# Cross and FFN attention scores from SBUF in fp32 at four row positions, in a three-layer decoder kernel on one Trainium2 core

## The reference

```python
scores = jnp.einsum('bhtd,bhsd->bhts', q, k) + bias      # cross; FFN: / sqrt(8), no bias
probs = jax.nn.softmax(scores, axis=-1)
attn = jnp.einsum('bhts,bhsd->bhtd', probs, v)
attn = attn.reshape(B, T, E)                             # cross: heads NOT moved back:
return attn @ Wo.T + bo                                  # row r of the result mixes 16 query rows of one head
```

## Time and profile before

| | us |
|---|---|
| median of 3 runs | 501.8 (501.21 to 505.19) |
| the profiled execution's own time | 496.74 |
| its span, first to last instruction | 495.0 |
| mean granted TensorE clock, share of full speed | 0.906 |
| busy: PE, weight load, DVE, ACT, POOL | 372.0, 313.7, 292.6, 197.8, 185.8 |

### The profile page before, as it was taken

The page is one execution under the profiler, slowest core; times in us unless marked ns, Lnnn a source line. Parts: engine busy times, 40 slices in busy tenths (PEclk is TensorE's granted clock), DMA queues, the critical chain, the costliest instruction groups (busy, mean ns, idle before and its releaser), DMA issues.

```text
span 495.0 us, 12557 instructions
## 1 busy us (share of the span) xinstructions
PE 372.0 (75%) x4671; PEld 313.7 (63%) x4683; DVE 292.6 (59%) x838; ACT 197.8 (40%) x390; POOL 185.8 (38%) x249
## 2 busy tenths in 40 slices
PE   1699997387699889978999984993886950039995
PEld 0244453257698788977988973982875930039994
DVE  5323334379768778687876764683783645007773
ACT  1266666043233423434335453461652720015552
POOL 6773412102324343244535544044030322723554
PEclk9999999589899999999999988896995985559998
DMA  7102357625976868776415368659496000332431
GB/s 177 31 3 86 98 171 186 168 73 139 242 187 180 206 182 221 207 189 181 122 47 156 110 173 222 170 147 226 118 253 176 3 0 22 106 98 57 106 92 30
DMA packets 60003, 66.34 MB, mean 134 GB/s; under 512 B 4373, under 2 KB 47384, under 8 KB 57640
## 3 DMA queue, kind: packets, MB, share of 16 engines
q1 hardware_dynamic: 49992, 45.61, 35.5%
q10 hardware_dynamic: 8448, 16.78, 12.3%
q0 software_dynamic: 1504, 3.16, 1.8%
HBM read 46.77 MB, written 19.22 MB: 133 GB/s over the span
## 4 chain that ended last, share of the span: by engine, by line
PE 42%; DMA 19%; DVE 15%; issue 9%; POOL 8%; SPq 3%; ACT 1%; POOLq 0%; DVEq 0%; ACTq 0%
PE score_banks L537 18%; DMA stack<-k_scratch 15%; PE proj_bank L537 7%; PE out_bank L537 5%; PE finish_bank L540 4%; DMA k_scratch<-parts 3%; PE prep_bank L537 3%; POOL routed_rows L520 3%; DVE biased L968 3%; DVE rowmax L972 2%; PE score_banks L540 2%; PE prep_bank L540 2%; POOL parts L380 2%; SPq L269 2%; DVE rest L946 2%
## 5 line engine op out<-in xcount | busy, mean ns | idle before, releaser
L537 PE MATMUL score_banks<-stack 72*128 72x128 bf16 x1024 | 134.1, 228 | 38.5 <-DMA stack<-k_scratch 37.0
L815 ACT ACTIVATE probs<-score_banks 128x512 f32<-128x512 f32 x128 | 76.4, 597 | 116.4 <-PE score_banks L537 115.3
L537 PEld LDWEIGHTS score_banks<-stack 72*128 72x128 bf16 x1024 | 86.7, 103 | 41.8 <-issue 38.6
L537 PE MATMUL score_banks<-maxT,pick 128*128 128x128 bf16 x512 | 93.9, 225 | 0.0
L424 POOL TENSOR_TENSOR att_sel<-att,in_block 128x1024 f32<-128x1024 f32 x16 | 34.4, 2150 | 78.6 <-DVE att L1004 78.6
L540 PE MATMUL score_banks<-ident,bias_in 128*128 128x128 f32 x256 | 62.0, 278 | 0.0
L977 DVE TENSOR_REDUCE rowmax<-score_banks 128x4 f32<-128x512 f32 x64 | 41.5, 682 | 23.1 <-PE score_banks L537 23.1
L537 PEld LDWEIGHTS score_banks<-maxT,pick 128*128 128x128 bf16 x512 | 52.2, 102 | 4.4
L367 POOL TENSOR_SCALAR vareps<-meanvar 128x2 f32<-128x2 f32 x32 | 7.2, 225 | 124.7 <-DVE meanvar L921 124.7
L968 DVE TENSOR_TENSOR biased<-score_banks,bias_in 128x512 f32<-128x512 f32 x64 | 43.7, 683 | 16.5 <-PE score_banks L537 15.9
L998 DVE RECIPROCAL rowsum_inv<-finish_bank 128x16 f32<-128x16 f32 x48 | 12.2, 255 | 68.4 <-PE finish_bank L540 68.2
(11 more groups left out here) (147 smaller groups left out, 655.2 us busy)
## 6 DMA issues: line engine op xcount, KB each, us to landing
k_scratch<-parts SPq DMA_DIRECT2D x48, 192.0 KB, 2.8
stack<-q_scratch SPq DMA_DIRECT2D x16, 576.0 KB
stack<-k_scratch SPq DMA_DIRECT2D x16, 576.0 KB
bias_in<-in_w SPq DMA_DIRECT2D x16, 256.0 KB, 8.2
q_scratch<-parts SPq DMA_DIRECT2D x16, 192.0 KB, 2.7
routed_rows<-filler SPq DMA_DIRECT2D x2, 1028.0 KB, 8.5
vaug<-routed_rows SPq DMA_DIRECT2D x23, 64.5 KB, 2.2
parts<-routed_rows SPq DMA_DIRECT2D x23, 64.0 KB, 2.1
```

Of the source, the lines that this page charges most:

```text
L537: return nc.tensor.matmul(o, lhsT, rhs, start=start, stop=stop, **kw)
L815: nc.scalar.activation(probs[:, b % 2, g, :], sbk[g % 2], ACT.Exp, scale=1.0 if layer(b) == CROSS else SCALE).then_inc(s_p, 1)
```

## The change

- The scratch round trip, the three bf16 parts and the stack go. q and k stay transposed in SBUF in fp32 (`qT`, `kT`), ScalarE takes them from PSUM with their biases (`take_qk`), and GpSimd multiplies them by the lane mask (`masked_keys`; for FFN `masked_queries` as well). All layers now use `row_products`, the form of the self layer.
- Cross scores are made once, as (query, key). VectorE adds the bias (1024 columns a time) and reduces; GpSimd subtracts the maxes (`subtract_maxes`), and TensorE transposes the 16 results (`cross_scores`). FFN scores are still made twice, and 16 products of 32 partitions subtract the maxes.
- Values are packed: two heads share 32 output columns, so the output bank has 256 columns and two transposes finish a batch instead of four.
- PSUM: six banks rotate as three pairs between exponentials and maxes, and one `work` and one `small` bank serve all else, guarded by `claim`. All exponentials take 1024 columns.
- The cross attention goes to DRAM in head order (`write_attention`, runs of 32 bytes) and back as rows (`read_attention`), is transposed, and meets Wo in one product. The projection comes 4 slots after the scores (3 from slot 36 on) instead of 2.
- The order within a slot changes on every engine, and there is one slot more. The tail is the same but for the gate's logits, which are now taken pair by pair.

The core of the diff:

```diff
+def pair_turns():
+    turns = []
+    for b in range(NB):
+        turns += [("exp", b, 0), ("exp", b, 1)]
+        if FIRST_CROSS <= b + 2 < NB:
+            turns += [("max", b + 2, 0), ("max", b + 2, 1)]
+    return {turn: n % 3 for n, turn in enumerate(turns)}
+
+
+PAIR_BANKS = pair_turns()
...
+            def write_attention(c):
+                sp.wait_ge(s_att, c + 1)
+                if c - 2 >= FIRST_CROSS:
+                    sp.wait_ge(s_attr[c % 2], 16 * ((c - 2 - B) // 2 + 1))
+                sp.dma_start(att_scratch[c % 2].rearrange("h t d -> t h d"),
+                             att[:, c % 2, :].rearrange("p (h d) -> p h d", d=HD)).then_inc(s_attw[c % 2], 16)
...
+            def masked_keys(q):
+                i = q % NRING
+                pool.wait_ge(s_qkT, q - CROSS_PAIR + 1)
+                pair_done(pool, q - NRING)
+                mask_lanes(k_lane[:, i, :, :], kT[:, i, :]).then_inc(s_klane, 1)
+
+            def masked_queries(q):
+                i = q % NRING
+                mask_lanes(q_lane[:, i, :, :], qT[:, i, :]).then_inc(s_qlane, 1)
+
+            def subtract_maxes(b, half):
+                i, u, two = b % 2, 2 * (b - B) + half, slice(2 * half, 2 * half + 2)
+                pool.wait_ge(s_rmax, u + 1)
+                v = biased[:, i, two, :].rearrange("p g (h k) -> p (g h) k", k=S)
+                nc.gpsimd.tensor_tensor(v, v, rowmax[:, i, 8 * half:8 * half + 8].unsqueeze(2).to_broadcast([128, 8, S]),
+                                        ALU.subtract).then_inc(s_sub, 1)
 
             def self_values(q):
...
+            let_go = {}
+
+            def claim(bank):
+                if bank in let_go:
+                    pe.wait_ge(*let_go[bank])
+
...
+            def row_products(kind, b, still, moving, start):
...
+                    done.append(mm(bank_of(kind, b, g).rearrange("p (h k) -> p h k", h=G),
+                                   still[rows_of, i, s * S:(s + 1) * S], moving[rows_of, i, :, s * S:(s + 1) * S],
+                                   start=start, stop=kind == "max" or layer(b) == SELF, tile_position=(G * HD * g, 0)))
...
+            def cross_scores(b):
+                for half in range(2):
+                    claim(PAIR_BANKS["exp", b, half])
+                    pe.wait_ge(s_sub, 2 * (b - B) + half + 1)
+                    for g in (2 * half, 2 * half + 1):
+                        for h in range(G):
+                            last = tr(bank_of("exp", b, g)[:, h * S:(h + 1) * S], biased[:, b % 2, g, h * S:(h + 1) * S])
+                    last.then_inc(s_e, 1)
...
+            def ffn_scores(b):
...
+                row_products("exp", b, kT, q_lane, start=True)
+                pe.wait_ge(s_maxT, b - FIRST_FFN + 1)
                 for h in range(G):
+                    for g in range(NG):
+                        rows_of = slice(G * HD * g, G * HD * (g + 1))
+                        last = mm(bank_of("exp", b, g)[:, h * S:(h + 1) * S], pick[rows_of, h, :],
+                                  maxT[rows_of, b % 2, :], start=False, stop=h == G - 1, tile_position=(G * HD * g, 0))
...
             def out_transposed(b):
+                claim("small")
                 pe.wait_ge(s_out, b + 1)
...
+                for two in range(2):
+                    last = tr(small[:, two * S:(two + 1) * S], outT[:, two * S:(two + 1) * S])
                 last.then_inc(s_otr, 1)
+                let_go["small"] = s_att, b + 1
...
             def out_projected(b):
+                claim("small")
+                pe.wait_ge(s_attT, b - B + 1)
+                mm(small[:, 0:D], attT[:], wx["xo" if layer(b) == CROSS else "fo"][:]).then_inc(s_oproj, 1)
+                let_go["small"] = s_res, b + 1
...
+                if b < NB:
+                    (self_scores, cross_scores, ffn_scores)[layer(b)](b)
+                if 0 <= b - 2 < NB:
+                    out_transposed(b - 2)
                 if 0 <= b - 1 < NB:
                     add_outputs(b - 1)
+                if FIRST_CROSS <= b + 2 < NB:
+                    score_maxes(b + 2)
+                if FIRST_FFN <= b + 1 < NB:
                     max_transposed(b + 1)
+                if b % 2 == 1 and CROSS_PAIR <= q + 3 < NP:
+                    qk_products(q + 3)
                 if b % 2 == 0 and CROSS_PAIR <= q + 2 < NP:
                     v_products(q + 2)
+                if c is not None:
+                    attention_transposed(c)
                 if b % 2 == 0 and q + 3 < NP:
                     transposes(q + 3)
+                if c is not None:
+                    out_projected(c)
...
...
+            def row_maxes(b, half):
...
                     dve.wait_ge(s_mp, u + 1)
...
+                    nc.vector.tensor_tensor(biased[:, i, two, :], banks,
...
                     dve.wait_ge(s_mfree, u + 1)
+                    nc.vector.tensor_reduce(peak, biased[:, i, two, :].rearrange("p g (h k) -> p (g h) k", k=S),
                                             AX.X, ALU.max).then_inc(s_rmax, 1)
...
+                if 0 <= b - 2 < NB:
+                    attention(b - 2)
                 if b % 2 == 0 and q + 3 < NP:
                     norm_stats(q + 3)
...
+                if FIRST_FFN <= b + 1 < NB:
                     take_maxT(b + 1)
                 if maxes:
                     row_maxes(b + 2, 0)
-                    row_maxes(b + 2, 1)
                 if b % 2 == 0 and CROSS_PAIR <= q + 2 < NP:
                     take_values(q + 2)
                 if b % 2 == 0 and q + 3 < NP:
                     normalise(q + 3)
...
                 if maxes:
+                    row_maxes(b + 2, 1)
+                    if layer(b + 2) == FFN:
+                        max_parts(b + 2)
+                if projected_first(b) is not None:
+                    residual(projected_first(b))
```

More of the change, by code:

```diff
@@ new lines, in score_maxes, with max_transposed @@
+            def score_maxes(b):
+                for half in range(2):
+                    claim(PAIR_BANKS["max", b, half])
+                pe.wait_ge(s_klane, b // 2 - CROSS_PAIR + 1)
+                done = row_products("max", b, qT, k_lane, start=True)
+                for half in range(2):
+                    done[2 * half + 1].then_inc(s_mp, 1)
+                    let_go[PAIR_BANKS["max", b, half]] = s_mfree, 2 * (b - B) + half + 1
+            def max_transposed(b):
+                claim("small")
+                pe.wait_ge(s_mparts, b - FIRST_FFN + 1)
+                nc.tensor.transpose(small[:].bitcast(bf16)[:, 0:128], maxparts[:], identb[:]).then_inc(s_mtr, 1)
+                let_go["small"] = s_maxT, b - FIRST_FFN + 1
```

611 lines of the change are left out of this document (250 added, 361 removed).

## The result

The changed kernel takes 532.4 us (median of 4 runs, 527.6 to 537.5) against 501.5 (500.8 to 505.2) for the kernel before, measured beside it: 1.059 times as long, 95% interval 1.054 to 1.065. Its profiled execution has a span of 529.8 us against 495.0. The forecast was 485, and its range of 8 in 10 went from 447 to 532.

A forecast was written before the change was run, and what follows sets the result against it. TensorE's work and stack waits bound the old kernel; order inside the slot would decide the new one. Stretches with norm waits and clock charges summed to a 478 us span, 479.7 with 1.7 outside, times 1.010 giving 485; range 447 to 532.

The forecast's parts named there:

- VectorE's 4.8 a slot for the maxes: Cross slots: bias and reduce of 1024 columns take VectorE 2.4 us a half, both halves 4.8, as before.
- the odd cross slot: Odd cross slot with a projection: 7.5 us to the next score products, whose output transposes wait for the residual.
- L: Even slots: VectorE's norm waits for GpSimd, about 1.6 us in cross (0 to 3.4), 0.9 in FFN (0 to 2.7).
- The clock in self and FFN: TensorE standing still in even slots costs clock: 0.6 us charged in self, 1.0 in FFN, against 1.9 in cross.
- The odd FFN slots: FFN stage, slots 32 to 45: 6.55 us for each of 7 odd slots.
- The steps of the even cross slot: From one start of the score products to the next, an even cross slot with a projection takes 8.45 + L us.
- FFN's 7.25 and 6.55: FFN stage: an even slot takes 7.25 us plus L, an odd slot 6.55.
- the 17.5 of slots 30 and 31: Slots 30 and 31, which take FFN maxes, were put at 17.5 us.
- the 1.5 us for reading the attention back: SyncE's DMA round: 6.9 us for the attention write to land plus 1.5 for the read, 8.4 a slot, no cost.
- the second rival: Cross slots run mostly at 1.2 GHz because transposes may not hold the clock: 57 us more, 542 or 520; chance 0.18.
- The first (clock holds, norm does not wait): No clock charge gives 457 us, without the norm's wait for GpSimd as well 437; chance 0.25.
- The third: Attention write's 32-byte runs cost twice a 512-byte run, SyncE's round 15.3 us a slot, about 565 us; chance 0.07.

The follow-up runs named there:

- e7: Changed kernel with GpSimd making the lane masks in the odd slot instead of the even slot where VectorE normalises; 531.9 us, 1.056 of the kernel before.
- e1: Changed kernel with VectorE's norm of pair q+3 moved ahead of the first half of the row maxes and the value copy; 536.2 us, 1.076 of the kernel before.
- e4: Changed kernel with identity products added on TensorE while it waits for xn, 14 in a cross pair, 8 in others; 508.0 us, 1.012 of the kernel before.
- e11: Changed kernel with transposes of the identity added on TensorE while it waits for xn, 14 in cross, 8 elsewhere; 510.0 us, 1.013 of the kernel before.
- e8: e6 with VectorE adding the residual ahead of the second half of the row maxes; 433.9 us, 0.860 of the kernel before.
- e5: Changed kernel with statistics ahead of the attention, norm and value copy ahead of the first half of the maxes; 480.5 us, 0.954 of the kernel before.
- e12: e8 with ScalarE instead of VectorE normalising pairs 3 to 23, first in the even slot; 436.2 us, 0.864 of the kernel before.
- e6: Changed kernel re-ordered so pairs' statistics, norm, transposes and values come a slot earlier, masks after the norm; 447.7 us, 0.891 of the kernel before.

## Why the prediction was wrong

The span was forecast as 478 and came as 529.8, 52 more; by its own stretches, from first exponentials: to slot 1 +2.9 (23.24 for 20.3), slots 1 to 13 +9.8, 14 to 20 +8.1, 21 to 29 +6.2, 30 and 31 +5.1, 32 to 45 +16.0 (125.95 for 110), to the gate +5.3 (442.1 - 413.8 = 28.3 for 23), tail -1.3 (87.7 for 89).

**The mechanism was right, its sizes and with them the direction were not.** The bound was the order in the slot, where it was put: even slots, TensorE behind the norm, the norm behind GpSimd, self slower than before, even and odd slots alternating. VectorE's 4.8 a slot for the maxes was 4.9 (1.22 an instruction, forecast 1.2), the output transposes wait 0.77 for the residual, the odd cross slot took 7.7 from products to products (7.5 forecast), and no DMA binds.

**The term that failed first is L**, "about 1.6; the bounds are 0, and 3.4 if the second norm instruction waits for the next mask too". It did wait: 3.59 - 0.6 = 3.0 in cross, and in FFN 2.84 - 0.6 = 2.2 for the 0.9, as in this pair:

```profile
345.88 1.89 POOL L381 TENSOR_TENSOR k_lane<-kT,in_lane 128x1024 f32<-128x1024 f32 x1
...
346.86 2.84 DVE L924 TENSOR_SCALAR xn<-x_sb,meanvar,rstd 128x128 f32<-128x128 f32 x2
...
347.73 1.89 POOL L381 TENSOR_TENSOR q_lane<-qT,in_lane 128x1024 f32<-128x1024 f32 x1
```

The row at the start had shown only the first of two waits, since one mask was all that GpSimd had queued there; here a subtraction and a mask, or two masks, are queued when the norm comes, and the second starts between the two norm instructions. The unfavourable bound was nearly the ordinary case, and in the terms of the sum it is worth 8 x 1.4 + 5 x 1.3 = 18 us of the 52 (only the even slots 32 to 40 of FFN norm a pair). That is the term's share, not what its removal gives: e7 and e1 took 12 and 24 us of the norm's waiting away in slots 14 to 31 and gained 4.5 and 12.6 there; the claim on `work` (e1) and the other waits of the slots took the rest.

**The clock in self and FFN was undersized.** Cross was about right (3.2 us at half in the slot shown, 1.6 for the 1.9; its 16 transposes took 2.96 us, in the other even slots up to 3.62). In self I charged 0.6 and e4 and e11 measure 1.5 to 1.9. I had made the loss smaller with the shorter stillness (2.6 us against 4.3), but the work at half speed behind it was as long after either (3.0 us at 0.50 in self, 3.2 at 0.51 in cross). Twice the lower clock lasted into the odd slot too: it was 0.50 from 30 to 36 us, and slots 3 and 7 took 4.3 us where e11's took 3.4. From slot 2 to 14 e11 needs 63.8 us where the changed kernel needed 74.5, 10.7 us for the 6 x 0.6 = 3.6 charged, which is 7 of the 9.8 us of self; by e4, with 68.2 us and longer slots 10 and 12, it is 3. In FFN the mean clock of 0.89 over 125 us is 27.5 us' worth at half speed, so at most 2.0 us a pair for the 1.0 charged.

**The odd FFN slots** took 8.0 for 6.55, 10 us together: slot 35 projects two batches (9.6), and slots 43 and 45 already carry a last norm (9.2, 8.9). In slot 43 its transposes wait 1.80 us at 393.44 for `work`, which the copy of the logits, last in VectorE's slot, lets go: one more claim of the same kind. I had let these norms begin at 46, though `LAST_NORMS` begins at 42. In the 28.3 for 23 at the end the same claim costs 0.56 and 2.64 us in two slots; the rest is not accounted for.

**Smaller slips of the working.** The steps of the even cross slot add up to 8.29 + L, not 8.45; FFN's 7.25 and 6.55 and the 17.5 of slots 30 and 31 (22.6 measured) are not laid out step by step; no row gives the 1.5 us for reading the attention back, which landed in 1.8; and half of the second rival's 57 us gives 514, not 520.

**The sign** follows from these. The margin forecast was 3%, made of terms that are each taken between ends, and L and the clock in self stood nearer their favourable end than the runs did.

**The rivals.** The first (clock holds, norm does not wait) needs an order that this kernel lacks. e8 comes out at 434 where the rival's lower end said 437, but that nearness is chance: e8 has another order, its norm pair still takes 1.9 to 2.2 us in five cross pairs, and its mean clock is 0.900. The second named 520 to 542 and the time fell there, which is chance as well, since it did not come by its mechanism: transposes hold the clock in self (e11), and the 16 of each odd cross slot from 17 to 29 ran in the 1.91 us of the higher clock. The third is refuted by the landing in 4.3 us.

What stays open: why FFN gains nothing in e5 and loses in e12, and the first 2.9 us. No run was made for them.

## What to carry to other kernels

When two banks serve what four did, write down for each claim which instruction of which queue lets it go, and look at whether two of them stand at the same place: moving one alone gained nothing (e1), moving both and the statistics within the slot gained 52 us (e5), and moving them a slot earlier 85 (e6), with 14 more for an earlier residual (e8). A leaner kernel can be slower only because its engines wait for each other once a pair; the signs here are two large idle sums that name each other while no engine is over 80% busy. Of a wait that the trace shows once, ask how long the queue behind the other engine is now, and take the bound that this gives.

## What the runs showed of the hardware

- Two VectorE norms of 0.3 us each wait for two different GpSimd instructions: 3.59 us in a row for 0.6, whether written with scalars or with two tensors (1744 and 1808 ns at the median of one). The reduce of 1024 fp32 columns in SBUF (1.22 us) and additions with one tensor in PSUM (0.28) kept their time beside a busy GpSimd.
- Work added while TensorE would stand still shortened the kernel by 24 us with products and 22 with transposes. In self both held the granted clock at 1.00, where it was 0.75 from 40 to 60 us.
- A write of 2048 runs of 32 bytes landed in 4.3 us, and none of VectorE's or TensorE's waits from 118 to 288 us, in cross, ended with a DMA.
